# Layer-2 self-attention: the softmax sums are spread by one product and inverted as a whole bank on VectorE

## Chip, core and metric

One NeuronCore of a Trainium2 chip runs the whole program, a four-layer decoder. The metric is the device time of one execution in microseconds (us). Engines are named as in the profile: PE is TensorE (PEld its weight loads), DVE is VectorE, ACT is ScalarE, POOL is GpSimd, SP is SyncE.

## The reference

The program computes twelve sublayers in a row on x of 4 x 512 x 256. The change touches one of them, the self-attention of layer 2:

```python
x = x + _L2_attn_ref(_layernorm(x), Wq, bq, Wk, bk, Wv, bv, Wo, bo, attn_scale)   # among 12 sublayers
...
def _L2_attn_ref(x, Wq, bq, Wk, bk, Wv, bv, Wo, bo, attn_scale):
    CHUNK = 64
    HEADS = 16
    B, T, C = x.shape                                  # 4, 512, 256
    q = (x @ Wq.T + bq).reshape(B, T, H, D)            # D = 16
    k = (x @ Wk.T + bk).reshape(B, T, H, D)
    v = (x @ Wv.T + bv).reshape(B, T, H, D)
    scores = jnp.einsum('bqhd,bkhd->bhqk', q, k) * attn_scale[0]
    mask = _chunk_mask(T, CHUNK)                       # causal, from chunks of 64 and the place in a chunk
    scores = jnp.where(mask[None, None], -jnp.inf, scores)
    attn = jax.nn.softmax(scores, axis=-1)
    out = jnp.einsum('bhqk,bkhd->bqhd', attn, v).reshape(B, T, C)
    return out @ Wo.T + bo
```

What matters is the last step of the softmax: the sum of the exponentials of each head and query divides that head's 16 output values.

## The kernel before

`l2_attn` works batch by batch (4 batches) and inside a batch by groups of 4 heads (GR = 4), so there are 16 groups. Heads are padded to 32 rows, so 4 heads fill 128 partitions. The stage is laid out in slots n; four slots make a group, one for each tile of 128 queries (TILE = 0, 3, 2, 1), and each engine has one hand-written loop over the slots that fixes its order. Semaphores are all that joins the engines.

In slot n TensorE computes the scores of item n (`score`, L1886), whose width is 512, 128, 256 and 384 in turn. VectorE masks them and takes the row maxima (`row_max`, L2101 and L2105, two pairs of heads one behind the other). Seven slots later TensorE computes the transposed scores with the maximum taken off (`score_T`, L1899), ScalarE takes the exponentials (L1962) and GpSimd cuts masked ones to zero (L2008, L2011). Scores and transposed scores share six PSUM banks as three pairs (`pair_banks`): a product into a pair waits until the row maximum or the exponential has read what stood there. Banks 6 and 7 serve everything else, one unit after the other; `emptied` is TensorE's wait for the reader of the unit that stood in the bank.

At slot n = 4q + 11 (`attend_at`) group q is finished: `attend` (L1913) multiplies probabilities and values into bank 6. The values have a column of ones as number 16 of each head's 32, so row 32h + 16 of the result holds head h's sums, and the other rows its unscaled outputs. ScalarE copies the bank into `attended_sums_T` (ou, L1984). Then, before the change:

- "pick", bank 7, behind the items of slot 4q + 11: four products (L1832) with ou as the weights and the four sum-selecting columns of the constant `spread_sums` as the moving side give 128 x 16 sums, queries on partitions. VectorE inverts them (L2081) ahead of the row maxima of the next slot.
- ScalarE copies the 16 inverses, each 32 times, into `inv_sum_wide` (L1974).
- "spread", bank 6, behind slot 4q + 12: four turns (L1838) bring them back to 128 rows by 512 queries. VectorE multiplies ou by the bank (L2086) into `attended_T`, behind the row maxima of slot 4q + 13.

`spread_sums` is 128 x 128 and holds, for each head, a row of 32 ones at row 32h + 16, over that head's 32 columns.

In slot 4q + 12 TensorE first computes the scores (512 wide), then for twelve of the sixteen groups (q = 0 to 11) the key projection of a later group (L1814 with `Wk`) into bank 7. That is the bank of the pick, so `emptied` makes it wait for `inverted`, the semaphore of the reciprocal. Behind the key projection stands the 128-wide `score_T`, then the spread, then the 128-wide scores of slot 4q + 13, the 512-wide `score_T` and the query projection (L1814 with `Wq`) into bank 6. For q = 12 to 15 there is no key projection there, and from slot 64 on there are no scores and no row maxima.

## Time and profile before

| | |
|---|---|
| median of 3 runs | 3920.9 us (3913.72 to 3924.44) |
| profiled execution | 3895.01 us, its span 3893.3 us |
| busy over the whole span | PE 3471.5 us (89%), DVE 2192.1 us (56%), ACT 1506.5 us (39%), POOL 1392.1 us (36%) |
| this stage, 1574 to 1948 us | 374 us; PE 314.61, DVE 213.94, ACT 116.42, POOL 104.23 us busy |
| mean granted clock of PE | 0.932 over the span, 0.90 in the stage |
| DMA | mean 28 GB/s over the span; almost none in the stage |

The granted clock is a share of 2.4 GHz; 0.50 is the lower of its two levels, 1.2 GHz, and a value between is a mean over a stretch that has both. A row of the timeline gives the start, the length, engine, line, operation and count of a run of equal instructions, and in brackets how long the engine had been idle before it and what ended that. Ends of matmuls are modelled, so neighbours overlap by some hundredths of a microsecond.

### The profile page before, as it was taken

How to read it: one execution, taken by the hardware profiler on the slowest of the kernel's cores; microseconds unless marked ns; L12 is line 12 of the kernel's file. 1: busy time of each engine (PE TensorE's matmuls, PEld its weight loads, DVE VectorE, ACT ScalarE, POOL GpSimd, SP SyncE). 2: the span in 40 equal slices, each digit the busy share in tenths (PEclk: the TensorE clock that was granted, in tenths of full speed). 3: DMA queues.
4: the chain of work that ended last, by engine and by line, in shares of the span. 5: the costliest groups of instructions: out<-in, count | busy, mean ns of one | idle time of the engine just before them, and what ended most of it. 6: DMA issues, size and time to landing. Idle time of an engine off the chain costs nothing. (4 is left out here: it accounts for less than half of the span.)

```text
span 3893.3 us, 54516 instructions
## 1 busy us (share of the span) xinstructions
PE 3471.5 (89%) x18930; PEld 2243.6 (58%) x18930; DVE 2192.1 (56%) x5349; ACT 1506.5 (39%) x3064; POOL 1392.1 (36%) x1928
## 2 busy tenths in 40 slices
PE   7998897999999978788888999999896979997996
PEld 5675684445555557344444555556794445555996
DVE  6374444646555558666367676765434456665454
ACT  2253102434434265133344444443453134443453
POOL 2141441423223245233244445443423134443412
PEclk9999978999999988899889999999898889997998
DMA  2005001000000000000010000000421000003312
GB/s 101 1 1 125 15 1 46 1 1 1 1 1 1 13 1 1 24 1 1 1 49 1 1 1 1 1 1 1 165 90 60 1 29 1 1 1 112 126 57 83
DMA packets 48720, 108.86 MB, mean 28 GB/s; under 512 B 6660, under 2 KB 32900, under 8 KB 46404
## 3 DMA queue, kind: packets, MB, share of 16 engines
q1 hardware_dynamic: 40964, 84.88, 6.6%
q0 software_dynamic: 7488, 20.49, 1.5%
q8 instruction: 158, 2.59, 0.3%
q14 instruction: 110, 0.90, 0.1%
HBM read 70.67 MB, written 34.68 MB: 27 GB/s over the span
## 5 line engine op out<-in xcount | busy, mean ns | idle before, releaser
L2655 POOL TENSOR_SCALAR probs<-probs,inv_sum 128x512 f32<-128x512 f32 x640 | 438.2, 698 | 997.2 <-DVE inv_sum L2776 996.9
L2618 ACT ACTIVATE probs<-psum_banks,neg_max 128x576 f32<-128x576 f32 x640 | 468.5, 737 | 733.2 <-DVE neg_max L2861 733.2
L2861 DVE TENSOR_REDUCE neg_max<-psum_banks 128x1 f32<-128x576 f32 x640 | 455.0, 752 | 209.4 <-PE psum_banks L2493 202.8
L2493 PE MATMUL psum_banks<-keys_T,queries_T 64*128 64x288 f32 x2560 | 405.7, 436 | 52.5 <-ACT probs L2618 43.2
L2785 DVE COPY probs_T<-psum_banks 128x512 f32<-128x512 f32 x640 | 409.0, 680 | 4.2 <-PE psum_banks L2411 4.2
L2493 PEld LDWEIGHTS psum_banks<-keys_T,queries_T 64*128 64x128 f32 x2560 | 223.8, 189 | 268.8 <-ACT probs L2618 147.7
L2411 PE MATMUL psum_banks<-ident,probs 128*128 128x128 f32 x2560 | 357.6, 284 | 3.3 <-POOL probs L2655 2.4
L2411 PEld LDWEIGHTS psum_banks<-ident,probs 128*128 128x128 f32 x2560 | 281.2, 143 | 129.2 <-POOL probs L2655 75.2
L2443 PE MATMUL psum_banks<-probs_T,values 128*64 128x512 f32 x1280 | 311.3, 608 | 2.2 <-issue 2.2
L4419 PE MATMUL psum_banks<-sorted_T,tile_weights 128*128 128x128 f32 x2208 | 266.9, 278 | 0.0
L4419 PEld LDWEIGHTS psum_banks<-sorted_T,tile_weights 128*128 128x128 f32 x2208 | 259.5, 195 | 0.1
L2857 DVE TENSOR_TENSOR psum_banks<-psum_banks,key_mask 128x128 f32<-128x128 f32 x192 | 57.5, 299 | 273.3 <-PE psum_banks L2493 273.3
L2667 POOL TENSOR_TENSOR square_sum<-square_sum,neg_half 128x8 f32<-128x8 f32 x102 | 167.0, 1639 | 69.8 <-DVE square_sum L2751 68.3
L4318 POOL DMA_INDIRECT expert_outputs<-expert_rows,output_index x92 | 89.7, 975 | 268.6 <-DVE expert_rows L4703 115.8
L4435 PE MATMUL psum_banks<-w_L_experts_down,hidden_T 128*128 x736 | 174.3, 380 | 2.2 <-DVE expert_rows L4703 1.4
L2346 PE MATMUL psum_banks<-w_L_xattn_Wkv,batch_normed_T 128*128 128x512 f32 x320 | 156.3, 612 | 0.0
L2443 PEld LDWEIGHTS psum_banks<-probs_T,values 128*64 128x64 f32 x1280 | 78.9, 137 | 134.0 <-issue 123.2
L4500 ACT COPY tile_weights<-w_L_experts_up 128x1024 f32 (+1 forms) x92 | 135.3, 1472 | 22.9 <-issue 22.9
L4435 PEld LDWEIGHTS psum_banks<-w_L_experts_down,hidden_T 128*128 128x128 f32 x736 | 132.8, 190 | 17.2 <-issue 2.9
L1962 ACT ACTIVATE probs_T<-psum_banks 128x512 f32<-128x512 f32 (+3 forms) x128 | 83.0, 701 | 127.4 <-PE psum_banks L1899 126.5
L2658 POOL TENSOR_TENSOR context_probs<-probs,inv_sum 128x128 f32<-128x128 f32 x320 | 128.7, 402 | 0.0
L2618 ACT ACTIVATION_READ_ACCUMULATOR probs<-psum_banks,neg_max 128x1 f32 x640 | 125.4, 196 | 0.0
(538 smaller groups left out, 6160.1 us busy)
## 6 DMA issues: line engine op xcount, KB each, us to landing
normed<-sorted_rows SPq DMA_DIRECT2D x30, 385.5 KB, 3.4
sorted_rows<-zero_rows SPq DMA_DIRECT2D x8, 1028.0 KB, 16.6
w_L_experts_down<-in_L_experts_down SPq DMA_DIRECT2D x2, 4096.0 KB, 20.4
normed<-expert_outputs SPq DMA_DIRECT2D x8, 1024.0 KB, 6.9
w_L_xattn_Wkv<-in_L_xattn_Wkv SPq DMA_DIRECT2D x2, 2048.0 KB, 8.3
w_L_experts_up<-in_L_experts_up SPq DMA_DIRECT2D x1, 4096.0 KB, 12.2
sorted_rows<-zero_rows SPq DMA_DIRECT2D x4, 899.5 KB, 15.9
x_res<-in_x SPq DMA_DIRECT2D x4, 512.0 KB, 6.7
```

The lines of the kernel that those rows point to most:

```text
L2346: last = pe.matmul(k.ps[:, 7, :], rows, wkv[:, c, W + a * 512:W + (a + 1) * 512], start=c == 0, stop=c == KC - 1)
L2411: last = pe.transpose(k.ps[:, 4 + n % 2, c * P:(c + 1) * P], prob[:, (b * NS + s) % PB, at + c * P:at + (c + 1) * P], k.ident[:, :])
L2443: last = pe.matmul(k.ps[r, 6, :], values[:, b % VB, c, (2 * j + h) * 64:(2 * j + h + 1) * 64], pT[:, q % 2, h, c, :], start=c == 0, stop=F ...
L2493: last = pe.matmul(k.ps[:, 2 * h + a, 0:HALF], qT[r, b % 2, j, t * P:(t + 1) * P], kT[r, j, k0:k0 + HALF], start=True, stop=True)
L2618: act.activation(prob[:, g % PB, h * w:(h + 1) * w].rearrange("p (a n) -> p a n", a=2), k.ps[:, 2 * h:2 * h + 2, 0:HALF], ACT.Exp, bias=nm ...
L2655: pool.tensor_scalar(w, w, inv[:, g % 4, h:h + 1], 1.0, ALU.mult, ALU.mult).then_inc(shared, 1)
L2667: pool.tensor_tensor(ss[:, i % 4, 2, :], ss[:, i % 4, 1, :], k.half[:, 0:8], ALU.pow).then_inc(inverted, 1)
L2785: dve.tensor_copy(pT[:, q % 2, h, :, t * P:(t + 1) * P], k.ps[:, 4 + n % 2, :].rearrange("p (c q) -> p c q", q=P)).then_inc(copied, 1)
L2861: dve.tensor_reduce(nmax[:, g % 4, h:h + 1], k.ps[:, 2 * h:2 * h + 2, 0:HALF], AX.XY, ALU.max, negate=True).then_inc(maxed, 1)
L4419: last = pe.matmul(ps[:, 2 * (n % 2) + part, f * P:(f + 1) * P], wt[:, n % 2, c, part * 512 + f * P:part * 512 + (f + 1) * P], xsT[:, n % ...
L4435: last = pe.matmul(ps[:, 6, 0:D], h[:, n % 2, f * P:(f + 1) * P], w_down[:, f // F, f % F * D:f % F * D + (E - 1) * STEP + D][:, bass.ds(a ...
L4500: act.copy(wt[:, n % 2, :, :], w_up[:, :, 0:(E - 1) * STEP + UP][:, :, bass.ds(at, UP)]).then_inc(weights_copied, 1)
```

## The change

The pick is now a single product with the whole of `spread_sums` as weights and ou as the moving side. Each head's sum lands on all 32 rows of that head, 128 x 512, in bank 7. VectorE takes the reciprocal of the whole bank into `inv_sum_wide` and multiplies ou by it at once. The four pick products, ScalarE's copy, the four turns, the spread unit and the small `inv_sum` tile go. Both VectorE instructions stand behind the row maxima of slot 4q + 12; before, the reciprocal stood ahead of these and the product one slot later.

```diff
--- before.py
+++ after.py
@@ -1715,9 +1715,7 @@
         va = k.sb("values_and_ones", [P, 2, TT, W], st)
         pT = k.sb("probs_T", [P, 8, 2, T], st)
         ou = k.sb("attended_sums_T", [P, 2, T], st)
-        inv = k.sb("inv_sum", [P, 2, HG * TT], st)
         wide = k.sb("inv_sum_wide", [P, T], st)
-        sum_rows = spread[:, :].rearrange("p (h d) -> p h d", d=32)[:, :, 0]
         oT = k.sb("attended_T", [P, 2, GR, T], st)
         ps = k.ps
         x = lambda b, t: k.x[:, TT * b + t, :]
@@ -1756,8 +1754,6 @@
                 return [("max", b, (n - 6) // 4, 6)]
             if attend_at(n) is not None:
                 return [("pick", b, attend_at(n), 7)]
-            if attend_at(n - 1) is not None:
-                return [("spread", b, attend_at(n - 1), 6)]
             return []
 
         def score_op(n):
@@ -1783,9 +1779,9 @@
                 keys_loaded, loaded, ones_set, stats, aggr, shift, rstd, normed, x_turned, x_moved, k_projected, k_made,
                 q_projected, q_made, v_projected, v_half, v_made), signals(
                 nc, "scored", "masked", "maxed", "max_turned", "max_added", "scored_T", "exped", "cut_late", "cut",
-                "attended", "summed_out", "picked_out", "inverse_copied", "spread_out", "inverted", "shared", "biased", "out_made", "out_added") as (
+                "attended", "summed_out", "sums_spread", "inverted", "shared", "biased", "out_made", "out_added") as (
                 scored, masked, maxed, max_turned, max_added, scored_T, exped, cut_late, cut, attended, sums_copied,
-                sums_picked, inverse_copied, sums_spread, inverted, shared, biased, out_made, out_added), nc.Block() as block:
+                sums_spread, inverted, shared, biased, out_made, out_added), nc.Block() as block:
 
             @block.sync
             def _(sp):
@@ -1828,16 +1824,8 @@
                         last.then_inc(max_turned, 1)
                     elif kind == "pick":
                         pe.wait_ge(sums_copied, i + 1)
-                        for t in range(TT):
-                            last = pe.matmul(ps[:, bank, HG * t:HG * t + HG], ou[:, i % 2, t * P:(t + 1) * P], sum_rows,
-                                             start=True, stop=True)
-                        last.then_inc(sums_picked, 1)
-                    elif kind == "spread":
-                        pe.wait_ge(inverse_copied, i + 1)
-                        for t in range(TT):
-                            last = pe.transpose(ps[:, bank, t * P:(t + 1) * P], wide[:, t * P:(t + 1) * P],
-                                                k.ident[:, :])
-                        last.then_inc(sums_spread, 1)
+                        pe.matmul(ps[:, bank, :], spread[:, :], ou[:, i % 2, :], start=True,
+                                  stop=True).then_inc(sums_spread, 1)
                     else:
                         pe.wait_ge(shared, GR * (b + 1))
                         for t in (2 * i, 2 * i + 1):
@@ -1860,8 +1848,6 @@
                         pe.wait_ge(max_added, i + 1)
                     elif kind == "pick":
                         pe.wait_ge(inverted, i + 1)
-                    elif kind == "spread":
-                        pe.wait_ge(shared, i + 1)
                     elif kind == "attend":
                         pe.wait_ge(sums_copied, i + 1)
                     else:
@@ -1966,14 +1952,6 @@
                 unit("turn", 0, 1, 6)
                 unit("key", 0, 0, 5)
                 for n in range(SLOTS):
-                    if attend_at(n - 1) is not None:
-                        q = attend_at(n - 1)
-                        act.wait_ge(inverted, q + 1)
-                        if q:
-                            act.wait_ge(sums_spread, q)
-                        act.copy(wide[:, :].rearrange("p (n d) -> p n d", d=32),
-                                 inv[:, q % 2, :].unsqueeze(2).to_broadcast([P, HG * TT, 32])).then_inc(
-                                     inverse_copied, 1)
                     for u in between(n):
                         unit(*u)
                     if attend_at(n) is not None:
@@ -2075,15 +2053,14 @@
                         dve.tensor_tensor(qm[:, g, :], qT[:, i // GR % 2, g, :], ps[:, bank, :],
                                           ALU.add).then_inc(max_added, 1)
                     elif kind == "pick":
-                        dve.wait_ge(sums_picked, i + 1)
-                        if i >= 2:
-                            dve.wait_ge(inverse_copied, i - 1)
-                        dve.reciprocal(inv[:, i % 2, :], ps[:, bank, 0:HG * TT]).then_inc(inverted, 1)
-                    elif kind == "spread":
                         dve.wait_ge(sums_spread, i + 1)
+                        if i:
+                            dve.wait_ge(shared, i)
+                        dve.reciprocal(wide[:, :], ps[:, bank, :]).then_inc(inverted, 1)
+                        dve.wait_ge(inverted, i + 1)
                         if i >= 2 * GR and i % GR == 0:
                             dve.wait_ge(out_made, 2 * (i // GR - 1))
-                        dve.tensor_tensor(oT[:, i // GR % 2, i % GR, :], ou[:, i % 2, :], ps[:, bank, :],
+                        dve.tensor_tensor(oT[:, i // GR % 2, i % GR, :], ou[:, i % 2, :], wide[:, :],
                                           ALU.mult).then_inc(shared, 1)
                     elif kind == "out":
                         dve.wait_ge(out_made, 2 * b + i + 1)
@@ -2118,12 +2095,12 @@
                 for n in range(SLOTS):
                     b, s = n // PER, n % PER
                     for u in behind(n - 1):
-                        if u[0] != "spread":
+                        if u[0] != "pick":
                             unit(*u)
                     if n < ITEMS:
                         row_max(n)
                     for u in behind(n - 1):
-                        if u[0] == "spread":
+                        if u[0] == "pick":
                             unit(*u)
                     for u in between(n):
                         unit(*u)
```

VectorE at group q = 7 (slot 40), before. The block mask and `neg_max` rows are two pairs of heads; the first four are the 512-wide item of slot 4q + 12, the next four the 128-wide one of slot 4q + 13. RECIPROCAL is the pick's, `attended_T` the final multiplication.

```order
L2081 RECIPROCAL inv_sum<-psum_banks 128x16
L2101 TENSOR_TENSOR psum_banks<-psum_banks,w_block_mask 128x2x128
L2105 TENSOR_REDUCE neg_max<-psum_banks 128x2
L2101 TENSOR_TENSOR psum_banks<-psum_banks,w_block_mask 128x2x128
L2105 TENSOR_REDUCE neg_max<-psum_banks 128x2
L2101 TENSOR_TENSOR psum_banks<-psum_banks,w_block_mask 128x2x128
L2105 TENSOR_REDUCE neg_max<-psum_banks 128x2
L2101 TENSOR_TENSOR psum_banks<-psum_banks,w_block_mask 128x2x128
L2105 TENSOR_REDUCE neg_max<-psum_banks 128x2
L2086 TENSOR_TENSOR attended_T<-attended_sums_T,psum_banks 128x512
L2054 TENSOR_SCALAR queries_T<-psum_banks,feature_vectors 128x512
```

The same place after:

```order
L2078 TENSOR_TENSOR psum_banks<-psum_banks,w_block_mask 128x2x128
L2082 TENSOR_REDUCE neg_max<-psum_banks 128x2
L2078 TENSOR_TENSOR psum_banks<-psum_banks,w_block_mask 128x2x128
L2082 TENSOR_REDUCE neg_max<-psum_banks 128x2
L2059 RECIPROCAL inv_sum_wide<-psum_banks 128x512
L2063 TENSOR_TENSOR attended_T<-attended_sums_T,inv_sum_wide 128x512
L2078 TENSOR_TENSOR psum_banks<-psum_banks,w_block_mask 128x2x128
L2082 TENSOR_REDUCE neg_max<-psum_banks 128x2
L2078 TENSOR_TENSOR psum_banks<-psum_banks,w_block_mask 128x2x128
L2082 TENSOR_REDUCE neg_max<-psum_banks 128x2
L2032 TENSOR_SCALAR queries_T<-psum_banks,feature_vectors 128x512
```

The reciprocal went from ahead of the first four to behind them and from 16 to 512 columns, and the multiplication from behind eight rows to right behind the reciprocal.

TensorE at the same group, before, from the pick on:

```order
L1832 MATMUL psum_banks<-w_spread_sums,attended_sums_T 128x4 x4
L1886 MATMUL psum_banks<-keys_T,queries_T 128x512 x4
L1814 MATMUL psum_banks<-batch_normed_T,w_L_padded_Wk 128x512 x2
L1899 MATMUL psum_banks<-queries_below_max_T,keys_T 128x128 x4
L1838 MATMUL psum_banks<-ident,inv_sum_wide 128x128 x4
L1886 MATMUL psum_banks<-keys_T,queries_T 128x128 x4
L1899 MATMUL psum_banks<-queries_below_max_T,keys_T 128x512 x4
L1814 MATMUL psum_banks<-batch_normed_T,w_L_padded_Wq 128x512 x2
L1886 MATMUL psum_banks<-keys_T,queries_T 128x256 x4
```

And after, where `w_spread_sums` are the weights and `attended_sums_T` moves:

```order
L1827 MATMUL psum_banks<-attended_sums_T,w_spread_sums 128x512
L1872 MATMUL psum_banks<-keys_T,queries_T 128x512 x4
L1810 MATMUL psum_banks<-batch_normed_T,w_L_padded_Wk 128x512 x2
L1885 MATMUL psum_banks<-queries_below_max_T,keys_T 128x128 x4
L1872 MATMUL psum_banks<-keys_T,queries_T 128x128 x4
L1885 MATMUL psum_banks<-queries_below_max_T,keys_T 128x512 x4
L1810 MATMUL psum_banks<-batch_normed_T,w_L_padded_Wq 128x512 x2
L1872 MATMUL psum_banks<-keys_T,queries_T 128x256 x4
```

Four products became one and the turns of `inv_sum_wide` are gone; the key projection (`w_L_padded_Wk`) still stands right behind the 512-wide scores and still waits for the reciprocal through bank 7.

## Rows read from the trace of the kernel before

**Rows 1.** The stage: us; PE, PEld, DVE, ACT, POOL busy; PEclk; DMA share, GB/s.
```profile
1574.00:1948.00 374.00, 314.61 (x2144) 157.15 (x2144) 213.94 (x388) 116.42 (x184) 104.23 (x280) 0.90 0.00 1
```

**Rows 2.** Waits in the stage: who for whom, total us, times, longest.
```profile
PEld psum_banks L1814 <- DVE attended_T L2086: 13.3, 12, 1.5
...
PEld psum_banks L1814 <- DVE inv_sum L2081: 9.1, 12, 0.8
```

**Rows 3.** Timeline of TensorE at group 7, from the pick on.
```profile
1778.66 1.03 PE L1832 MATMUL psum_banks<-w_spread_sums,attended_sums_T 128*128 128x4 f32 x8 [0.15 <-ACT attended_sums_T L1984]
...
1779.62 1.14 PE L1886 MATMUL psum_banks<-keys_T,queries_T 32*128 32x512 f32 x8
...
1780.69 1.98 PE L1814 MATMUL psum_banks<-batch_normed_T,w_L_padded_Wk 128*128 128x512 f32 x4
...
1782.67 0.50 PE L1899 MATMUL psum_banks<-queries_below_max_T,keys_T 32*128 32x128 f32 x8
...
1783.10 0.66 PE L1838 MATMUL psum_banks<-ident,inv_sum_wide 128*128 128x128 f32 x4
...
1784.17 0.50 PE L1886 MATMUL psum_banks<-keys_T,queries_T 32*128 32x128 f32 x8 [0.42 <-DVE neg_max L2105]
...
1785.78 1.82 PE L1899 MATMUL psum_banks<-queries_below_max_T,keys_T 32*128 32x512 f32 x8 [1.11 <-DVE neg_max L2105]
...
1787.54 2.95 PE L1814 MATMUL psum_banks<-batch_normed_T,w_L_padded_Wq 128*128 128x512 f32 x4
```

**Rows 4.** Timeline of VectorE at the same group.
```profile
1780.83 0.43 DVE L2101 TENSOR_TENSOR psum_banks<-psum_banks,w_block_mask 128x256 f32<-128x256 f32 x1 [0.84 <-PE psum_banks L1886]
...
1782.89 1.23 DVE L2105 TENSOR_REDUCE neg_max<-psum_banks 128x2 f32<-128x1024 f32 x1
...
1785.21 0.42 DVE L2105 TENSOR_REDUCE neg_max<-psum_banks 128x2 f32<-128x256 f32 x1
...
1786.35 0.68 DVE L2086 TENSOR_TENSOR attended_T<-attended_sums_T,psum_banks 128x512 f32<-128x512 f32 x1
```

**Rows 5.** VectorE's groups by form: busy us, mean ns of one, idle before.
```profile
L2776 DVE RECIPROCAL inv_sum<-exp_sum 128x2 f32<-128x2 f32 x320 | 48.9, 153 | 14.4 <-ACT probs L2618 14.4
...
L4668 DVE TENSOR_TENSOR hidden_T<-hidden_T 128x512 f32<-128x512 f32 x46 | 31.8, 692 | 96.8 <-ACT hidden_T L4524 96.8
...
L2105 DVE TENSOR_REDUCE neg_max<-psum_banks 128x2 f32<-128x512 f32 x32 | 22.2, 693 | 1.1
...
L2081 DVE RECIPROCAL inv_sum<-psum_banks 128x16 f32<-128x16 f32 x16 | 4.1, 257 | 34.6 <-PE psum_banks L1832 34.6
L3741 DVE RECIPROCAL key_sums<-key_sums 128x16 f32<-128x16 f32 x16 | 4.0, 253 | 0.6
...
L4615 DVE RECIPROCAL gate_total<-gate_total 128x12 f32<-128x12 f32 x2 | 0.5, 228 | 0.1
```

**Rows 6.** Single microseconds of the stage, columns as in rows 1.
```profile
1786.00:1787.00 1.00, 1.00 (x8) 0.09 (x4) 0.99 (x2) 0.00 (x0) 0.00 (x0) 0.55 0.00 0
1789.00:1790.00 1.00, 1.00 (x3) 0.25 (x1) 0.00 (x0) 0.59 (x1) 0.74 (x3) 0.74 0.00 0
1885.00:1886.00 1.00, 0.00 (x0) 0.00 (x0) 1.00 (x1) 0.00 (x0) 0.00 (x0) 0.55 0.00 0
1898.00:1899.00 1.00, 1.00 (x4) 0.80 (x3) 0.00 (x0) 0.00 (x0) 0.00 (x0) 0.63 0.00 0
```

**Rows 7.** Timeline of TensorE: a slow key projection, group 12, the last group.
```profile
1601.02 3.78 PE L1814 MATMUL psum_banks<-batch_normed_T,w_L_padded_Wk 128*128 128x512 f32 x4
...
1890.03 2.09 PE L1899 MATMUL psum_banks<-queries_below_max_T,keys_T 32*128 32x512 f32 x8 [1.11 <-DVE neg_max L2105]
...
1932.07 1.02 PE L1832 MATMUL psum_banks<-w_spread_sums,attended_sums_T 128*128 128x4 f32 x8 [0.80 <-ACT attended_sums_T L1984]
...
1935.68 8.83 PE L1845 MATMUL psum_banks<-w_L_padded_Wo,attended_T 128*128 128x256 f32 x32 [0.87 <-DVE attended_T L2086]
```

**Rows 8.** Timeline of VectorE: the widest row maxima of group 12.
```profile
1884.49 0.43 DVE L2101 TENSOR_TENSOR psum_banks<-psum_banks,w_block_mask 128x256 f32<-128x256 f32 x1 [0.84 <-PE psum_banks L1886]
```

## The prediction

> **What bounds the kernel now.** I read four views, from coarse to fine. First the busy times of the stretch from 1574 to 1948 us, the only one whose code changes: TensorE is busy for 314.61 of 374 us, VectorE for 213.94, ScalarE for 116.42 [rows 1]. TensorE sets the pace, but it is idle for 59 us, so some waits end on it. Second the waits of the stage: two of them are on the very instructions that the change moves. TensorE's key projection waits for the small reciprocal in 12 groups (9.1 us in total, 0.8 at the longest), the query projection for the final multiplication (13.3 us, of its weight loads) [rows 2]. Third the timelines of one group. TensorE runs pick, 512-wide scores, key projection, 128-wide score_T, turns nearly without a gap, then waits 0.42 us and 1.11 us for row maxima [rows 3]. VectorE begins the row maxima of the 512-wide item when its scores end and needs 3.29 us for them (1780.83 to 1782.89 + 1.23) [rows 4]. So TensorE is the bound, and behind the 512-wide scores it depends on VectorE within one or two instructions. Last the granted clock in single microseconds, since it halves in this stage: 0.55 at 1786 us, back up in the course of 1789 us [rows 6].
>
> The question is therefore not how much TensorE work goes, but when the reciprocal is done: bank 7 is free for the key projection only then.
>
> **The reciprocal.** No row shows one of 512 columns. The program's reciprocals last 153 ns for 2 columns, 228 for 12, 253 for 16, and 257 for 16 out of PSUM [rows 5]. From 12 to 16 columns that is 25 ns for 4, or 6.25 ns a column, so 512 columns would last 257 + 496 x 6.25 = 3357 ns. From 2 to 16 it is 100 ns for 14, or 7.1 ns: 3.80 us. The low end is a VectorE instruction that takes each column in one pass: 692 to 693 ns for 512 columns [rows 5]. I take 3.36 us: the slope between the two longest forms is the nearest to a long row, and a one-pass cost would have added 4 ns and not 25 between them. The Trainium skill (VectorE: DVE Perf Modes, First, the fixed hardware budget) says that Reciprocal is an iterated divide with a repeat count of 8 on the first slices of the pipe. The rows agree that it is no one-pass operation, but show a smaller factor; what eight passes would make is a rival below.
>
> **Groups 0 to 11, with a key projection.** Removed on TensorE: four products, 1.03 us from 1778.66, and four turns, 0.66 us [rows 3]. Added: one product of 512 columns. Four such projection products take 1.98 us, so it costs from 0.50 (a quarter) to 0.66 us (turns with as many columns in all) [rows 3]. I take 0.6. The 512-wide scores could start up to 0.4 us earlier; since exponentials may still hold their banks I take 0.3. Removed on ScalarE: a copy per group; its cover was ScalarE's idle time, and it is worth nothing except where named below.
>
> VectorE then starts the row maxima at 1780.5 instead of 1780.83 and ends them at 1783.8. Only now comes the reciprocal: 1783.8 + 3.36 = 1787.15. With 0.1 us for the semaphore the key projection starts at 1787.3, where it started at 1780.69 [rows 3, 4]: **+6.6 us**. Queued behind it on TensorE are the 128-wide score_T, the 128-wide scores, the 512-wide score_T and the query projection; nothing can pass. Two things come back: the turns (0.66) are gone, and the 0.42 us wait before the 128-wide scores too, as their pair of banks is free by then. The 1.11 us before the 512-wide score_T stays, since it follows those scores. Net **+5.5 us** a group. The final multiplication (0.68 us [rows 4]; the same for two SBUF operands, 0.692 [rows 5]) moves into VectorE's idle time while the key projection runs: nothing, and if that cover were gone 0.7. Could TensorE's idle time later in the group take up some of the 5.5? VectorE, ScalarE and GpSimd work on results of TensorE's items in order, and wait for them, so they shift along; I count nothing.
>
> **The clock.** TensorE would stand still from about 1780.4 to 1787.3, almost 7 us. In group 12 it fell to the lower level (0.5, that is 1.2 GHz) in the first fully idle microsecond behind the 512-wide scores [rows 6]. So I expect the key projection at 1.2 GHz. One such took 3.78 us instead of 1.98 [rows 7, 3]: **+1.8 us** a group. Low stretches that were followed by dense work lasted about 3.4 us (1786.1 to 1789.4 [rows 6]), so it should be over when the projection is. The query projection already pays for such a stretch in many groups (2.95 instead of 1.98 in this one [rows 3]), behind the same two short items and the 1.11 us wait; I leave that loss where it is. Ends: it vanishes (-0.95), or the low level holds on as it did from 1885 to 1898 us, some 13 us [rows 6].
>
> **Group 12** has row maxima behind it but no key projection. There 1884.49 - 0.3 + 3.29 + 3.36 + 0.68 puts the row maxima of the 128-wide item at 1891.5; the first half takes about 0.9, and the 512-wide score_T goes from 1890.03 to 1892.5 [rows 7, 8]: +2.5 us. **Groups 13 and 14** have no row maxima, so the reciprocal lies in VectorE's idle time, and TensorE is rid of turns and of 0.4 us of pick: -1 us each. **Group 15**: from the start of the pick to the output projection it takes 3.61 us now (1932.07 to 1935.68 [rows 7]); after it 0.6 + 3.36 + 0.69 and some 0.25 in semaphores, 4.9: +1.3 us.
>
> **The sum.** 12 x (5.5 + 1.8) = 87.6; + 2.5 - 2.0 + 1.3 gives **+89.4 us**. The profiled execution took 3895.0 us, so one like it would take 3984; the median of the runs shown is 3920.9, 26 us above that execution, and with the same difference I forecast **4010 us**.
>
> **Rivals.**
> - The low clock holds on (12%). After the stall TensorE gets one dense piece, then short items and a wait. If the level stays low for about 13 us, as in group 12, four more microseconds are lost per group: 4010 + 48 = 4058. Against it: there was no 3.8 us of dense work in group 12 behind the stall.
> - The clock costs nothing on balance (12%). The stall makes the low stretch fall into idle time, and the later one vanishes: 12 x (1.8 + 0.95) = 33 less, 3977.
> - Eight passes a column (8%). A one-pass row maximum gains 0.54 us from 512 to 1024 columns [rows 4, 5], 1.05 ns a column; eight times that is 8.4 ns, and the reciprocal lasts 257 + 496 x 8.4 = 4.42 us, 1.06 more in 14 groups: 4025. This is the skill's repeat count, taken literally.
> - A long reciprocal in one pass a column (5%): 2.67 us less in 14 groups, 37 in all: 3973. Even then the key projection waits for row maxima and reciprocal.
> - Faster (3%): TensorE never meets the wait. The price of the place is nil if the reciprocal ends before the 512-wide scores do, within 1.1 us of the product. Then 16 x (0.4 + 0.66) = 17 us of TensorE's work go: 3904. Against it stands VectorE's order, with 3.29 us of row maxima ahead of it in each of the 12 groups.
> - Swallowed (3%): the delay of 5.5 us disappears in TensorE's own gaps, 59 / 16 = 3.7 us a group, and what is left is paid by the removed work: 3921.
>
> **How the numbers follow.** The forecast gets 57%, with 3995 to 4030 as its own range. Slower by over 0.3% are the forecast, both clock cases and both other reciprocals: 94%. Within 0.3% (about 12 us, what a measurement of this kernel can tell from no change): 3%. Faster: 3%. The range runs from 3968 (the one-pass case less the 5 us by which runs differ) to 4054 (forecast, eight passes, half of the long low clock, 5 us of spread) and leaves out the last two cases and the upper half of the first.
>
> **What would show it.** In the profile after, the reciprocal's row gives its length: 3.3 to 3.8 us right, 0.7 or 4.4 for the rivals. TensorE's wait before the key projection, 12 times, should name the reciprocal and be 6 to 7 us long; if it is below 1 us the whole forecast is wrong. The key projection should last 3 to 3.8 us at a granted clock of 0.5 and the next query projection no more than now. The stage should last about 463 us instead of 374, with TensorE's busy time little changed and its idle time up by some 75 us. If the stage grows by less than 50 us, look for gaps that closed; if all else in the program moves, the base did.

## The result, and the profile after

The changed kernel took **4035.1 us**, median of 4 runs (4029.8 to 4039.6), against 3921.2 us (3913.7 to 3924.4) for the kernel before on the same chip: a ratio of 1.0291 [1.0275, 1.0307], or +114 us. Measured a second time it took 4028.2 against 3916.5 us, 1.0294 [1.0277, 1.0311]. The forecast was 4010, that is +89, with a range of 3968 to 4054. The direction, the mechanism and the range were right, and the price was 25 us too small.

The runs below come from five series, and the kernel before does not take the same time in each (medians from 3894.9 to 3921.2 us). So each version stands against the kernel before of its own series, and durations are compared within the stage that is changed.

The head of the page after, with the span and the busy times of the engines:

```profile
span 4031.4 us, 54148 instructions
...
PE 3505.0 (87%) x18770; PEld 2242.5 (56%) x18770; DVE 2239.6 (56%) x5349; ACT 1496.5 (37%) x3048; POOL 1388.8 (34%) x1928
```

The stage after, in the columns of [rows 1], to its new end (2062), and then the waits that hang on the moved reciprocal and those next in size on TensorE (who for whom, total us, times, longest):

```profile
1574.00:2062.00 488.00, 340.06 (x1984) 150.49 (x1984) 264.05 (x385) 107.51 (x168) 105.83 (x280) 0.79 0.01 2
```

```profile
PEld psum_banks L1810 <- DVE inv_sum_wide L2059: 90.0, 12, 7.5
PE psum_banks L1810 <- DVE inv_sum_wide L2059: 80.1, 12, 6.7
...
PE psum_banks L1885 <- DVE neg_max L2082: 25.1, 18, 4.4
...
PE psum_banks L1872 <- ACT probs_T L1948: 16.4, 29, 1.2
```

From its first key projection to its last addition to x the stage lasted 366.2 us before and 479.5 after: **+113.3 us**, the whole of what the medians show. The profiled executions themselves differ by 138 us (3895.0 and 4033.2). The other 25 lie outside the changed stage: the profiled execution of before was 26 us under the median of its runs. TensorE has 88 us more idle time in the stage (59 against 148) and 25 us more busy time, though it executes 160 instructions fewer. The granted clock of the stage fell from 0.90 to 0.79.

VectorE's two groups on the new path, by form:

```profile
L2059 DVE RECIPROCAL inv_sum_wide<-psum_banks 128x512 f32<-128x512 f32 x16 | 53.6, 3349 | 12.7 <-PE psum_banks L1827 12.7
...
L2063 DVE TENSOR_TENSOR attended_T<-attended_sums_T,inv_sum_wide 128x512 f32<-128x512 f32 x16 | 11.1, 695 | 0.6
```

Group 7 on TensorE after the change, to be laid beside [rows 3] (start, duration; idle time before and its releaser in brackets):

```profile
1844.81 1.10 PE L1827 MATMUL psum_banks<-attended_sums_T,w_spread_sums 128*128 128x512 f32 x2 [0.15 <-ACT attended_sums_T L1962]
...
1845.83 1.14 PE L1872 MATMUL psum_banks<-keys_T,queries_T 32*128 32x512 f32 x8
...
1853.65 3.78 PE L1810 MATMUL psum_banks<-batch_normed_T,w_L_padded_Wk 128*128 128x512 f32 x4 [6.67 <-DVE inv_sum_wide L2059]
...
1857.36 0.81 PE L1885 MATMUL psum_banks<-queries_below_max_T,keys_T 32*128 32x128 f32 x8
...
1858.76 0.81 PE L1872 MATMUL psum_banks<-keys_T,queries_T 32*128 32x128 f32 x8 [0.59 <-ACT probs_T L1948]
...
1860.67 2.09 PE L1885 MATMUL psum_banks<-queries_below_max_T,keys_T 32*128 32x512 f32 x8 [1.09 <-DVE neg_max L2082]
...
1862.69 3.78 PE L1810 MATMUL psum_banks<-batch_normed_T,w_L_padded_Wq 128*128 128x512 f32 x4
```

And the same place on VectorE, beside [rows 4]:

```profile
1849.11 1.23 DVE L2082 TENSOR_REDUCE neg_max<-psum_banks 128x2 f32<-128x1024 f32 x1
...
1850.25 3.35 DVE L2059 RECIPROCAL inv_sum_wide<-psum_banks 128x512 f32<-128x512 f32 x1
...
1853.63 0.69 DVE L2063 TENSOR_TENSOR attended_T<-attended_sums_T,inv_sum_wide 128x512 f32<-128x512 f32 x1
...
1859.63 0.43 DVE L2078 TENSOR_TENSOR psum_banks<-psum_banks,w_block_mask 128x256 f32<-128x256 f32 x1 [5.31 <-PE psum_banks L1872]
```

The chain is closed: the last wide row maximum ends at 1850.3, the reciprocal at 1853.6, and the key projection starts at 1853.65, 8.84 us after the start of the pick, where it was 2.03 before (1778.66 to 1780.69 [rows 3]). VectorE then waits 5.31 us itself for TensorE's next scores.

The granted clock (the third column from the right) in single microseconds of this group:

```profile
1849.00:1850.00 1.00, 0.00 (x0) 0.00 (x0) 0.97 (x2) 0.00 (x0) 0.00 (x0) 0.72 0.00 0
1852.00:1853.00 1.00, 0.00 (x0) 0.00 (x0) 1.00 (x1) 0.00 (x0) 0.00 (x0) 0.50 0.00 0
1864.00:1865.00 1.00, 1.00 (x2) 0.38 (x2) 0.00 (x0) 0.76 (x1) 0.79 (x3) 0.50 0.00 0
1866.00:1867.00 1.00, 1.00 (x9) 0.34 (x8) 0.49 (x1) 0.00 (x0) 0.00 (x0) 0.75 0.00 0
```

It falls while TensorE stands still (in the course of 1849 us), is 0.50 in every microsecond from 1850 to 1865, and comes back in the course of 1866: about 17 us at 1.2 GHz, the first four of them before the key projection begins. The key projection, the three short items and nearly the whole query projection fall into it.

### The profile page after: what moved, and what is told of

The parts are those of the page before. It is cut to its first block and busy times, and to the rows that moved or that the text cites. A ratio compares the mean times of both kernels' runs of the same rounds, so it can differ in the third digit from the quotient of the medians.

```text
span 4031.4 us, 54148 instructions
## 1 busy us (share of the span) xinstructions
PE 3505.0 (87%) x18770; PEld 2242.5 (56%) x18770; DVE 2239.6 (56%) x5349; ACT 1496.5 (37%) x3048; POOL 1388.8 (34%) x1928
## 5 line engine op out<-in xcount | busy, mean ns | idle before, releaser
L4412 PEld LDWEIGHTS psum_banks<-w_L_experts_down,hidden_T 128*128 128x128 f32 x736 | 134.9, 193 | 32.4 <-issue 17.4
L1986 POOL TENSOR_SCALAR_AFFINE_SELECT probs_T<-probs_T 128x128 f32<-128x128 f32 x128 | 37.2, 290 | 328.9 <-ACT probs_T L1948 326.7
```

Source lines behind the costliest of these rows:

```text
L4412: last = pe.matmul(ps[:, 6, 0:D], h[:, n % 2, f * P:(f + 1) * P], w_down[:, f // F, f % F * D:f % F * D + (E - 1) * STEP + D][:, bass.ds(a ...
```

## The experiments

Three questions were open after the result. Is it the wait for bank 7 alone? How is it shared between the reciprocal's length, its place behind the row maxima, and the clock? And can the new form, with less work on TensorE, be placed so that it costs nothing? Positive differences below are slower than before.

**e1_fill: work in TensorE's wait.** Thirteen products into bank 6, which is free, keep TensorE busy while the key projection waits.

```diff
+    FILL = 13
@@ TensorE, between the scores of slot n and the units behind them
+                    if attend_at(n - 1) is not None and attend_at(n - 1) < 12:
+                        for _ in range(FILL):
+                            pe.matmul(ps[:, 6, :], spread[:, :], ou[:, attend_at(n - 1) % 2, :], start=True, stop=True)
```

> The changed kernel with 13 extra products of 128x512 into bank 6 behind the 512-wide scores of each of the 12 groups with a key projection; nothing reads them. They fill the 6.67 us in which TensorE waits for the reciprocal. Theory A (the clock falls in that wait and costs 3.6 us a group behind it: key projection 1.8, short items 0.6, 512-wide score_T 0.6, query projection 0.65): the key projections last 1.98 us instead of 3.78 and the kernel takes about 3992 us (43 less than the changed kernel's 4035). Rival (the later items are slow for another reason, such as traffic on PSUM by VectorE's long instruction): the projections stay at 3.8 us and the time at 4035 or a little above.

Measured: 4028.3 against 3894.9 us, 1.0337 [1.0318, 1.0356], +133 us. The size was wrong: each product of 512 columns is two records, and the filling outlasted the wait.

```profile
1822.87 11.43 PE L1919 MATMUL psum_banks<-attended_sums_T,w_spread_sums 128*128 128x512 f32 x26
```

It took 11.4 us where the wait was 6.7, some 4.7 us too many 12 times, 57 us. The difference to the changed kernel is only 133 - 114 = 19, so 38 us must have come back from the clock. That was an inference, so it was run again at the right size.

**e5_fill7: seven products.** The same edit with `FILL = 7`.

> As e1_fill, with 7 extra products a group instead of 13. The trace of e1_fill shows each 128x512 product as two records of 0.44 us, so 13 took some 11.4 us and overran the wait of 6.67; 7 take 6.2 and fit. Theory A (clock): key projections of 1.9 us instead of 3.8, short items 0.6 and the 512-wide score_T 0.4 less, the query projection a little: 3.0 us a group, 36 in all, so the kernel before + 78 us. Rival (no clock effect on the time): the kernel before + 114 us.

Measured: 3997.7 against 3916.5 us, 1.0203 [1.0186, 1.022], **+81 us**. TensorE's timeline in one group:

```profile
1715.82 6.28 PE L1919 MATMUL psum_banks<-attended_sums_T,w_spread_sums 128*128 128x512 f32 x14
...
1722.57 1.98 PE L1811 MATMUL psum_banks<-batch_normed_T,w_L_padded_Wk 128*128 128x512 f32 x4 [0.47 <-DVE inv_sum_wide L2063]
...
1725.70 0.50 PE L1873 MATMUL psum_banks<-keys_T,queries_T 32*128 32x128 f32 x8 [0.71 <-ACT probs_T L1952]
...
1728.37 1.98 PE L1811 MATMUL psum_banks<-batch_normed_T,w_L_padded_Wq 128*128 128x512 f32 x4
```

The reciprocal ends as late as before, but the key projection takes 1.98 us in all 12 groups. So does this query projection; seven others are slow (2.6 to 3.7 us), and the twelve take 33.6 us together, near the 32.4 of the kernel before. The stretch from 1630 to 1900 us, of the kernel before, the changed kernel and e5_fill7 in turn:

```profile
1630.00:1900.00 270.00, 237.07 (x1704) 118.56 (x1704) 167.41 (x300) 92.07 (x146) 82.27 (x224) 0.93 0.00 1
```

```profile
1630.00:1900.00 270.00, 187.19 (x1097) 79.53 (x1098) 145.78 (x216) 60.81 (x96) 57.27 (x156) 0.78 0.00 1
```

```profile
1630.00:1900.00 270.00, 239.44 (x1365) 105.23 (x1364) 161.70 (x237) 66.51 (x105) 62.97 (x172) 0.96 0.00 1
```

The granted clock is 0.78 after, 0.96 with filling, and 0.93 before. The stage lasts 444.4 us with filling and 478.2 for the changed kernel in the same series. **The delay itself costs about 80 us, and the clock that the standstill loses about 34** (by the whole time 31 from the medians, 36 from the two ratios). In groups 0 to 11 alone, where the filling is, it is 36 (359.8 less 323.4 us); in the last groups e5_fill7 is 2.8 us slower. The forecast had 66 and 22 for groups 0 to 11.

**e2_bank6: another bank.** The pick's product goes to bank 6, so that the key projection does not wait for the reciprocal.

```diff
-                return [("pick", b, attend_at(n), 7)]
+                return [("pick", b, attend_at(n), 6)]
```

> The changed kernel with the spreading product in bank 6 instead of 7, so that the key projection (bank 7) no longer waits for the reciprocal. Theory A (bank 7 carries the stall, but the row maxima of the next slot still stand behind the reciprocal on VectorE): the key projection starts at once, the 512-wide score_T comes 3.0 us later than before the change instead of 5.5, with about 1.7 us of clock: 12 x 4.7 + 2 = +58 against the kernel before, 3979 us. Rival (VectorE's queue alone carries it, the bank is no matter): 4035 us.

Measured: 3950.9 against 3894.9 us, 1.0141 [1.0124, 1.0158], +56 us. TensorE's timeline:

```profile
1816.61 1.98 PE L1810 MATMUL psum_banks<-batch_normed_T,w_L_padded_Wk 128*128 128x512 f32 x4
...
1824.98 2.09 PE L1885 MATMUL psum_banks<-queries_below_max_T,keys_T 32*128 32x512 f32 x8 [4.38 <-DVE neg_max L2082]
```

The wait before the key projection is gone, and half of the loss with it. The other half meets TensorE a few items later: the next row maxima stand behind the long reciprocal in VectorE's queue, and the 512-wide `score_T` needs them. So the bank is not the whole cause. 3.35 us of VectorE at this place come to light on one path or the other.

**e4_copy: a short instruction in the reciprocal's place.** A copy of 512 columns takes its place. The division is left out.

```diff
-                        dve.reciprocal(wide[:, :], ps[:, bank, :]).then_inc(inverted, 1)
+                        dve.tensor_copy(wide[:, :], ps[:, bank, :]).then_inc(inverted, 1)
```

> The changed kernel with a one-pass copy of the bank in place of the reciprocal, so the sums are not inverted (the division is left out). Theory A (length and place add up): the copy lasts 0.68 us, the wait before the key projection falls from 6.67 to 4.0 us, 32 us less in 12 groups and up to 10 us of clock, 3993 to 4003 us, and so still 70 to 80 us above the kernel before, by place alone. Rival (the long reciprocal is the whole cost): within 12 us of the kernel before, 3909 to 3933 us.

Measured: 3975.5 against 3894.9 us, 1.0206 [1.0189, 1.0223], +80.5 us. Its waits in the stage:

```profile
PE psum_banks L1810 <- DVE inv_sum_wide L2059: 48.1, 12, 4.0
```

With the long reciprocal out of the way 4.0 of 6.67 us of each wait remain, and 80 of 114 us of the loss. The length alone is the smaller part. Most of it is that anything at all on which TensorE waits stands behind 3.3 us of row maxima.

**e6_big_ahead and e7_small_behind: length and place, one at a time.** The first is the changed kernel with the long reciprocal, and the final multiplication behind it (0.69 us), ahead of the row maxima. The second is the kernel before with its small reciprocal (0.25 us) behind them.

```diff
@@ e6_big_ahead, VectorE: all units ahead of row_max
                     for u in behind(n - 1):
-                        if u[0] != "pick":
-                            unit(*u)
+                        unit(*u)
                     if n < ITEMS:
                         row_max(n)
-                    for u in behind(n - 1):
-                        if u[0] == "pick":
-                            unit(*u)
@@ e7_small_behind, VectorE of the kernel before
-                        if u[0] != "spread":
+                        if u[0] not in ("pick", "spread"):
...
-                        if u[0] == "spread":
+                        if u[0] in ("pick", "spread"):
```

> The changed kernel with VectorE's long reciprocal and multiplication ahead of the row maxima of slot 4q + 12, where the small reciprocal stood before the change. Length without the place. Theory A: the key projection waits 2.5 us instead of 6.7, the row maxima end 3.0 us later than before the change, which sets the 128-wide scores and the 512-wide score_T; with 1.8 us of clock 4.8 a group, in 12 groups, and 2 to 4 elsewhere: the kernel before + 60 us. Rival (the order of two things that must both be done does not matter): + 114 us.

> The kernel before with one edit: its small reciprocal (128x16) stands behind the row maxima of slot 4q + 12 instead of ahead of them. Place without the length; four pick products, copy and turns stay. Theory A: the key projection waits 3.8 us, less the 0.42 us wait that goes, so 3.3 and 2.0 of clock, 5.3 a group: the kernel before + 64 us. Rival (only the long reciprocal costs): within 5 us of the kernel before.

Measured: e6_big_ahead 3966.7 against 3916.5 us, 1.0127 [1.011, 1.0145], +50 us; e7_small_behind 3975.7, 1.0154 [1.0138, 1.0171], +59 us. The long reciprocal ahead of the row maxima (VectorE, then TensorE):

```profile
1706.99 3.36 DVE L2059 RECIPROCAL inv_sum_wide<-psum_banks 128x512 f32<-128x512 f32 x1 [1.41 <-PE psum_banks L1827]
...
1710.40 3.53 PE L1810 MATMUL psum_banks<-batch_normed_T,w_L_padded_Wk 128*128 128x512 f32 x4 [2.38 <-DVE inv_sum_wide L2059]
```

The short one behind them:

```profile
1765.22 0.25 DVE L2081 RECIPROCAL inv_sum<-psum_banks 128x16 f32<-128x16 f32 x1
...
1765.52 3.78 PE L1814 MATMUL psum_banks<-batch_normed_T,w_L_padded_Wk 128*128 128x512 f32 x4 [3.58 <-DVE inv_sum L2081]
...
1774.20 1.98 PE L1814 MATMUL psum_banks<-batch_normed_T,w_L_padded_Wq 128*128 128x512 f32 x4 [0.16 <-DVE attended_T L2086]
```

Behind a wait of 2.4 us eleven of the 12 key projections took 2.4 to 3.6 us instead of 1.98 (one stayed at 1.98), and behind 3.6 us all 12 took 3.78. In e7_small_behind the low clock was over in time for the query projection: all 12 took 1.98 us, where before the change they took 2.7 in the mean.

The two parts, 50 for the length and 59 for the place, add up to 109 of 112 us in this series. That the two are independent is read from this sum alone: e6_big_ahead also has the multiplication ahead of the row maxima, e7_small_behind keeps the four small products, the copy and the turns, and the length alone is worth 34 us by e4_copy, where the place is the new one.

**e3_late: the product one slot later.** The pick stands behind slot 4q + 12, where no projection needs bank 7 soon, and VectorE inverts behind the row maxima of slot 4q + 13, which are short.

```diff
-            if attend_at(n) is not None:
-                return [("pick", b, attend_at(n), 7)]
+            if attend_at(n - 1) is not None:
+                return [("pick", b, attend_at(n - 1), 7)]
```

> The changed kernel with the spreading product one slot later, at the place of the turns that were removed, in bank 7 behind the key projection; VectorE's reciprocal and multiplication then stand behind the row maxima of the 128-wide item. Theory A (3.35 us of reciprocal cost nothing where no TensorE item is due: the next user of bank 7 is some 1.3 us later, and row maxima are not delayed): TensorE is rid of 1.0 us a group, 3905 to 3912 us, 9 to 16 below the kernel before. Rival (a reciprocal of this length always delays something on VectorE, here the query projection's or the next item's step): 3935 us or more.

Measured: 3920.0 against 3894.9 us, 1.0063 [1.0046, 1.008], +25 us. I had expected a gain of 9 to 16. The place removes most of the loss, but does not turn it round. Four rows of one group show why:

```profile
1775.31 1.14 PE L1872 MATMUL psum_banks<-keys_T,queries_T 32*128 32x512 f32 x8 [0.81 <-ACT probs_T L1948]
...
1785.76 3.32 DVE L2063 TENSOR_TENSOR attended_T<-attended_sums_T,inv_sum_wide 128x512 f32<-128x512 f32 x1
...
1785.76 2.76 POOL L1980 TENSOR_TENSOR x_res<-x_res,row_vectors 128x256 f32<-128x256 f32 x4
...
1792.30 1.66 PE L1885 MATMUL psum_banks<-queries_below_max_T,keys_T 32*128 32x384 f32 x8 [4.53 <-DVE neg_max L2082]
```

First, TensorE gains nothing by the move. The pick had stood between the 256-wide `score_T` and the 512-wide scores, and had covered a wait for ScalarE's exponentials. Without it TensorE waits 0.81 us there in every group, and only 0.3 of the pick's 1.0 us comes back. Second, the reciprocal now delays the row maxima of slot 4q + 14: TensorE waits 2.9 and 1.9 us for them in the first two groups (none to 0.6 in most of the others), and twice 1.7 us for the queries. Third, in three groups the multiplication begins in the same instant as GpSimd's bias addition and takes 3.32 us instead of 0.69; there the wait for row maxima was 4.53, 4.53 and 3.23. Before the change one operand came out of PSUM (0.68 us [rows 4]), and no multiplication ran at the same time as a bias addition; now both operands lie in SBUF and three coincide. The Trainium skill (SBUF — State Buffer, "SBUF: two separate sides") says that a VectorE operation with two SBUF inputs and a GpSimd operation that reads SBUF take turns on one pair of ports, and that the one that comes second is held up entirely. This trace agrees: 3.32 is about 2.76 + 0.69. The 2.76 us are four additions, so the multiplication did not get in between them either.

**e9_late_bias: e3_late without the collision.** The bias addition moves one slot.

```diff
-                    if s == 6 and b < B:
+                    if s == 7 and b < B:
                         add_bias(b)
```

> e3_late with GpSimd's bias addition one slot later. In e3_late the final multiplication, two operands in SBUF, began together with that addition in three groups and lasted 3.32 us instead of 0.69. Theory B (the two hold each other up at SBUF): all 16 multiplications last 0.69 us, and 8 of the 25 us by which e3_late stood above the kernel before go: before + 17 us. Rival (the long ones are waits for something else): they stay, and + 25 us.

Measured: 3903.9 against 3895.4 us, 1.0018 [1.0009, 1.0027], +7 to 8.5 us; the expected +17 was too much. By form and on the timeline:

```profile
L2063 DVE TENSOR_TENSOR attended_T<-attended_sums_T,inv_sum_wide 128x512 f32<-128x512 f32 x16 | 11.1, 692 | 0.5
```

```profile
1653.99 0.93 PE L1885 MATMUL psum_banks<-queries_below_max_T,keys_T 32*128 32x384 f32 x8 [2.88 <-DVE neg_max L2082]
```

All multiplications take 0.69 us again. The gain over e3_late was 17 us, where three times 2.6 us give 8. The timelines show where the rest lies. From the 512-wide scores of one group to those of the next, the three groups with the collision took 24.7, 26.1 and 25.0 us in e3_late and 21.0, 21.1 and 19.7 here, 14 us in all. About 9 of these are the shorter wait for row maxima; the other 5 are work at the lower clock behind the long wait (the 384-wide `score_T` in the last row shown for e3_late takes 1.66 us instead of 0.93). Another 3 us lie ahead of the first pick, where the two kernels are the same. The wait of 2.88 us in the first group remains, and so do 1.9 us in three others.

**e8_pieces: the reciprocal in two halves.** ScalarE copies the bank out, and VectorE inverts and multiplies 256 columns at a time, half of it one slot later (in the last group of a batch both at once), with the bias addition moved as well.

```diff
@@ TensorE, emptied
-                        pe.wait_ge(inverted, i + 1)
+                        pe.wait_ge(sums_moved, i + 1)
@@ ScalarE
+                        act.wait_ge(sums_spread, q + 1)
...
+                        act.copy(wide[:, :], ps[:, 7, :]).then_inc(sums_moved, 1)
@@ VectorE
-                    elif kind == "pick":
...
-                        dve.reciprocal(wide[:, :], ps[:, bank, :]).then_inc(inverted, 1)
+                    elif kind == "piece":
+                        r = slice(bank * (T // 2), (bank + 1) * (T // 2))
+                        dve.wait_ge(sums_moved, i + 1)
+                        dve.reciprocal(wide[:, r], wide[:, r]).then_inc(inverted, 1)
...
+                    q = attend_at(n - 2)
+                    if q is not None:
+                        unit("piece", 0, q, 0)
...
+                    q = attend_at(n - 3)
+                    if q is not None and q % GR != GR - 1:
+                        unit("piece", 0, q, 1)
```

> The changed kernel with the long reciprocal in two pieces off the chain: ScalarE copies the spread sums out of bank 7 (one copy a group, as before the change), so that bank is free at once; VectorE inverts and multiplies columns 0 to 255 behind the row maxima of slot 4q + 13, the others behind those of slot 4q + 14 (every fourth group both at the first place); GpSimd's bias addition one slot later. Theory A (3.35 us of reciprocal cost only what they hold up): no wait of TensorE for a reciprocal; the first piece, 2.1 us, fits into the 2.4 to 3.5 us in which VectorE waits for the query projection; TensorE is rid of 0.6 us a group: between 8 us below and 5 above the kernel before. Rival (VectorE's 3.8 us more a group hold up row maxima wherever they stand, as in e3_late): 15 us or more above the kernel before.

Measured: 3916.2 against 3895.4 us, 1.0049 [1.0035, 1.0063], +21 us, where -8 to +5 was expected. The halves by form, and its waits in the stage:

```profile
L2064 DVE RECIPROCAL inv_sum_wide<-inv_sum_wide 128x256 f32<-128x256 f32 x32 | 55.8, 1744 | 14.2 <-ACT inv_sum_wide L1960 14.2
```

```profile
PE psum_banks L1885 <- DVE neg_max L2087: 23.3, 20, 2.7
...
PE psum_banks L1899 <- DVE queries_below_max_T L2059: 13.5, 11, 4.2
```

Each half is shorter, but the second one meets another dependent: the reduced queries (`queries_below_max_T`), for which TensorE now waits 11 times. The longest of these waits, 4.2 us, stands behind a collision with the bias addition, which its new slot did not avoid here:

```profile
1788.18 3.10 DVE L2068 TENSOR_TENSOR attended_T<-attended_sums_T,inv_sum_wide 128x256 f32<-128x256 f32 x1
1788.24 2.76 POOL L1986 TENSOR_TENSOR x_res<-x_res,row_vectors 128x256 f32<-128x256 f32 x4
```

This multiplication of 256 columns takes 0.42 to 0.55 us elsewhere. By its record it began 0.06 us ahead of the addition and was held up all the same, so these starts do not tell which of the two gets the ports. Two interruptions of 2.2 us, with one collision and a copy on ScalarE, cost more here (21 us) than one of 4.0 in e9_late_bias (8 us).

**e10_late_share and e11_before_bias: what is left.** e10_late_share is e9_late_bias with the final multiplication one slot later in three of four groups. e11_before_bias is the kernel before with nothing but the moved bias addition, the control for that move in e8, e9 and e10.

```diff
@@ e10_late_share, VectorE: the unit in two, then their places
                         dve.reciprocal(wide[:, :], ps[:, bank, :]).then_inc(inverted, 1)
+                    elif kind == "share":
                         dve.wait_ge(inverted, i + 1)
...
-                    for u in behind(n - 1):
-                        if u[0] == "pick":
-                            unit(*u)
+                    for q, late in ((attend_at(n - 3), 1), (attend_at(n - 2), 0)):
+                        if q is not None and late == (q % GR < GR - 1):
+                            if not late:
+                                unit("pick", 0, q, 7)
+                            unit("share", 0, q, 7)
+                        elif q is not None and not late:
+                            unit("pick", 0, q, 7)
```

> e9_late_bias with VectorE's final multiplication (0.69 us) behind the row maxima of slot 4q + 14 instead of ahead of them, in three of four groups. In e9_late_bias TensorE still waits 1.9 to 2.9 us a group for those row maxima. Theory A (every microsecond of VectorE ahead of a row maximum that TensorE waits for is paid in full): 9 groups x 0.69 = 6 us less than e9_late_bias, so level with the kernel before (+ 1 us). Rival (the multiplication only moves the wait on to the next item): no gain, + 7 us.

> The kernel before with GpSimd's bias addition one slot later and nothing else, to see whether that move is worth anything by itself. Theory A (before the change the final multiplication read one operand from PSUM and lasted 0.68 us in all 16 groups, so there is nothing to gain): within 3 us of the kernel before. Rival (the move itself brought part of what e9_late_bias gained over e3_late): 5 to 9 us less than the kernel before.

Measured: e10_late_share 3921.4 against 3918.9 us, 1.0006 [0.9997, 1.0014], +2.4; e11_before_bias 3917.2, 0.9995 [0.9986, 1.0003]. The moved bias addition is worth nothing by itself, so what e9 wins over e3 by it is the collision that it avoids, and the rest of what e9 and e10 win over the changed kernel is due to the places of the product, the reciprocal and the multiplication. No version tried is quicker than the kernel before; the best one can't be told from it.

That e9 and e10 come so near has a second reason. Their twelve query projections take 24.6 and 23.8 us together, 1.98 us in nearly all groups, where the kernel before needs 32.4, since it runs seven of them in part or whole at the lower clock (2.95 us in [rows 3]). About 8 us of what the new form adds in waits is paid back in this way. Why the clock stays up there was not tested.

The ladder, in us against the kernel before of the same series:

| version | difference |
|---|---|
| wait overfilled (e1_fill) | +133 |
| changed kernel | +114, +112 |
| wait filled, clock kept (e5_fill7) | +81 |
| short instruction, same place (e4_copy) | +80.5 |
| small reciprocal, new place (e7_small_behind) | +59 |
| other bank (e2_bank6) | +56 |
| long reciprocal, old place (e6_big_ahead) | +50 |
| one slot later (e3_late) | +25 |
| reciprocal in two halves (e8_pieces) | +21 |
| one slot later, without the port collision (e9_late_bias) | +8 |
| and the multiplication later still (e10_late_share) | +2 |
| kernel before with the bias addition moved (e11_before_bias) | -2 |

## Why the prediction was right, and where it was off

**The reciprocal: right.** 3.36 us was forecast, and the sixteen have a mean of 3.35. The slope between 12 and 16 columns held to 512: (3349 - 257) / 496 = 6.23 ns a column. The rivals with 0.7 and 4.42 us are out. The Trainium skill (VectorE: DVE Perf Modes, "First, the fixed hardware budget") gives Reciprocal a repeat count of 8. Against the 1.05 ns a column of a one-pass operation the trace shows a factor of 5.9, so the count taken literally does not price it.

**The wait: right.** The forecast was a start of the key projection 6.6 us later behind VectorE, 12 times. It is 6.8 us later (8.84 less 2.03), with a wait of 6.67. The 0.1 us that the forecast allowed for the semaphore came from no row; here the key projection starts 0.05 us behind the end of the reciprocal. e2, e4, e6 and e7 each take one link out of the chain row maxima, reciprocal, bank 7, and each shortens the loss.

The times from one start to the next on TensorE, summed over groups 0 to 11 of the profiled executions, take the rest of the forecast apart (us):

| from | to | before | after | e5_fill7 |
|---|---|---|---|---|
| pick | key projection | 24.3 | 106.1 | 106.1 |
| key projection | 128-wide `score_T` | 23.7 | 44.0 | 23.0 |
| 128-wide `score_T` | 128-wide scores | 18.1 | 16.0 | 14.6 |
| 128-wide scores | 512-wide `score_T` | 19.3 | 21.0 | 19.2 |
| 512-wide `score_T` | query projection | 17.4 | 20.9 | 14.5 |
| query projection | 256-wide scores | 31.6 | 39.2 | 32.7 |
| 256-wide scores | next pick | 113.3 | 113.4 | 113.4 |
| sum | | 247.7 | 360.7 | 323.4 |

**What comes back: wrong, half of it.** The forecast let 1.08 us a group come back, since the turns (0.66) and the 0.42 us wait ahead of the 128-wide scores go. From the start of the 128-wide `score_T` to the start of the 128-wide scores it was 1.50 us (1782.67 to 1784.17 [rows 3]). It is 1.40 in the group shown, at the lower clock, and 1.21 in e5_fill7, where the clock is kept. So only 0.3 us comes back there. The turns had lain over ScalarE's exponentials of the `score_T` just issued, and with them gone TensorE waits 0.6 to 0.7 us for these. What the forecast did not count is 0.23 us more, mostly the 0.16 us wait for the final multiplication ahead of the query projection. With 0.06 us behind the key projection that is 0.6 us a group at the full clock: 7 us came back in 12 groups instead of 13, so **6 us** of the 25 missing ones are here. The prediction counted on the banks being free for the scores, and had not asked what is late next once the turns are out.

**The product: too small, and harmless.** 0.6 us was forecast, and it took 1.10. The four records of a projection in [rows 3] are two products of two records each and not four, so the "quarter" should have been a half. TensorE's saving on the pick was then nil and not 0.4 us, and the scores did not start 0.3 us earlier. The key projection was 6.8 and not 6.6 us later, 2.6 us over the 12 groups.

**The clock: right in kind, 16 us too small.** Forecast: key projections at 3.78 us, query projections as before, 22 us in all. Measured: nine key projections of 3.78, the others 3.50 to 3.75, together 44.9 us instead of 12 x 1.98 = 23.8, so +21 as forecast. The low level did not end with them, though, as the single microseconds of group 7 show. In eight groups it held on past the key projection; in the other four the 128-wide `score_T` was back at 0.50 us, but the 512-wide one behind it was slow again (1.5 to 1.9 us for 1.14). The twelve query projections grew from 32.4 us to 40.0 (2.7 to 3.3 each in the mean), and the short items between grew too. By the table the clock is worth 37 us against e5_fill7, and e5_fill7's query projections take 1 us more than those before: 38 us where the sum had 22. The forecast took the length of a low stretch from one that was followed by dense work [rows 6]. Here the dense piece was followed by items of 0.8 us and two waits. In e7_small_behind, after a wait of 3.6 us, the low stretch did end ahead of the query projection, so the forecast's picture is one that occurs; behind the wait of 6.7 us it came about in one group of 12 only (group 5, query projection 1.98 us). What decides between the two was not isolated. The rival "the low clock holds on" had the mechanism, at about a third of its extra 48 us.

**The small groups.** Group 12 cost 3.0 us (2.5 forecast), and groups 13 and 14 gave back 2.9 and 2.0 us from one pick to the next (1 each forecast). In group 15 the output projection starts 5.37 us after the pick instead of 3.61 and lasts 0.3 us longer, +2.0 (1.3 forecast). Together that is +0.1 where the sum had +1.8.

**The sum again.** In groups 0 to 11: 82 for the start, 38 for the clock and 7 less for what comes back are 113 us, the measured difference from the first pick to the thirteenth; the forecast had 79, 22 and 13, or 88. Of the 25 us between them 16 are the clock, 6 what did not come back and 3 the start. The small groups take 2 off, and the stage is 24 us above the forecast. That the total was still inside the range owes nothing to errors that cancelled: nearly all of them point the same way.

**The signs named in advance** were met but for three: the stage lasts 488 us in the same window and not 463, the query projection did not stay as it was, and TensorE's busy time grew by 25 us while its idle time grew by 88 instead of 75.

**Still open.** What makes the low clock end ahead of the query projection in all 12 groups of e7_small_behind and in one of the changed kernel; why the query projections keep the full clock in e9_late_bias and e10_late_share; and whether ScalarE, idle for three quarters of the stage, could compute the inverse from its tables without a loss, which wasn't tried.

## What to carry to other kernels

Count an instruction not by the TensorE work that it saves but by where its result is due: here some 9 us of removed TensorE work (pick 1.03 and turns 0.66 less 1.10, 16 times) stood against a path of row maxima and reciprocal in front of a bank that TensorE needed at once. The time of a reciprocal grows with the columns of its row, copies of one sum included: 16 columns cost 0.26 us and 512 cost 3.35. So invert the small form and spread afterwards, unless VectorE is idle there and nothing waits behind it. And when work is taken out of a busy engine, look for the wait that it covered (here twice: the turns, and the pick in e3_late); when an engine is made to wait, price the clock behind the wait too, beyond the next instruction.

## What the runs showed of the hardware

- VectorE's f32 reciprocal has a mean of 1744 ns for 256 columns and 3349 ns for 512, that is 6.3 ns a column between them. It is about five times a one-pass operation of the same width (692 ns).
- Dense work of 1.98 us took 2.4 to 3.6 us behind a wait of 2.4 us in 11 of 12 groups (e6_big_ahead), 3.78 us in all 12 behind one of 3.6 (e7_small_behind), and 3.5 to 3.8 behind one of 6.7 (the changed kernel). In group 7 of the latter 3.8 us of dense work did not bring the full rate back. Products without use in the wait kept the rate for the key projections, which was worth about 34 us.
- A VectorE multiplication of two SBUF operands that began together with four GpSimd additions took 3.32 us instead of 0.69 (three times in e3_late), and one of 256 columns 3.10 instead of 0.42 to 0.55 (e8_pieces), though by its record it began 0.06 us ahead of them.
